# One semaphore for each buffer of gathered rows in the first layer of a two-layer graph network

## The reference, cut to what matters

```python
src, dst = edge_index
h = relu(edge_attr @ W1 + b1)
w_edge = (h @ W2 + b2).reshape(-1, 16, 16)
msgs = einsum('ei,eio->eo', x[src], w_edge)      # x[src]: gathered rows
aggr = segment_sum(msgs, dst, num_segments=n_nodes)
```

## Time and profile before

| what | us |
|---|---|
| median of three runs | 8242.69 |
| lowest, highest | 8239.94, 8244.3 |
| span of the profiled execution, first to last instruction | 8221.3 |
| median less the span: what lies around it | 21.4 |
| first layer, gathers and all, from 60 to 4985 | 4925 |
| second layer's edge loop, about 5080 to 8130 | 3050 |

### The profile page before, as it was taken

One profiled execution on the slowest core, in us unless ns is written; L12 is line 12 of the kernel. 1 busy time (PEld: TensorE's weight loads), 2 busy tenths in 40 slices (PEclk: granted clock), 3 DMA queues, 4 the chain that ended last, 5 costly groups with the idle time before them and its releaser, 6 DMA issues. The chain is left out here.

```text
span 8221.3 us, 191064 instructions
## 1 busy us (share of the span) xinstructions
PE 7349.2 (89%) x52997; PEld 6446.6 (78%) x52997; DVE 6691.0 (81%) x17449; ACT 4457.4 (54%) x8279; POOL 5696.0 (69%) x4866
## 2 busy tenths in 40 slices
PE   7888888888888888888888886999999999999998
PEld 5667676666676666666676765999999999999996
DVE  6777777777777777777777777999999999999997
ACT  3333333333333333333333335888888878778884
POOL 6666666666666666666666664888888888888886
PEclk8999999999999999999999998999999999999999
DMA  2000000000000000000000014444444455554443
GB/s 60 18 17 17 17 17 17 17 17 17 17 17 17 17 18 17 17 17 18 17 17 17 17 23 101 73 75 74 74 75 74 74 73 74 72 74 75 73 75 64
DMA packets 713464, 341.73 MB, mean 42 GB/s; under 512 B 422115, under 2 KB 656599, under 8 KB 713427
## 3 DMA queue, kind: packets, MB, share of 16 engines
q1 hardware_dynamic: 379313, 272.94, 13.1%
q0 software_dynamic: 332928, 64.86, 12.9%
q10 hardware_dynamic: 1186, 3.51, 0.1%
HBM read 307.85 MB, written 32.96 MB: 41 GB/s over the span
## 5 line engine op out<-in xcount | busy, mean ns | idle before, releaser
L802 POOL DMA_INDIRECT xg<-gather_rows,idx x3132 | 3041.9, 971 | 1882.4 <-issue 1848.5
L919 PE MATMUL ps_w<-W2s,hT 128*128 128x256 f32 x12928 | 3240.2, 408 | 37.1 <-issue 36.6
L919 PEld LDWEIGHTS ps_w<-W2s,hT 128*128 128x128 f32 x12928 | 2678.5, 207 | 581.6 <-issue 97.0
L1745 POOL DMA_INDIRECT sums<-total,row x1616 | 2551.0, 1579 | 529.1 <-issue 474.4
L1708 PE MATMUL ps_wide<-hot_col,placed 128*128 128x392 f32 x12928 | 2434.7, 345 | 4.8 <-DVE placed L1544 2.1
L1708 PEld LDWEIGHTS ps_wide<-hot_col,placed 128*128 128x128 f32 x12928 | 2313.6, 196 | 12.2 <-issue 6.9
L841 ACT ACTIVATE hT<-ps_h,b1c 128x512 f32<-128x512 f32 x1616 | 1022.8, 680 | 2302.1 <-PE ps_h L905 2090.8
L1002 DVE TENSOR_TENSOR prod<-ps_w,xg 128x512 f32<-128x512 f32 x1616 | 1098.1, 690 | 969.7 <-remote 599.7
L1544 DVE SCALAR_TENSOR_TENSOR placed<-ps_r,src_r,halves 128x512 fp32r<-128x512 f32 x1616 | 1097.5, 741 | 0.1
L1643 ACT ACTIVATE square<-iota_col,minus_col 128x784 bf16<-128x784 int16 x1212 | 1061.3, 938 | 66.6 <-issue 58.0
L1009 DVE TENSOR_REDUCE msg<-prod 128x32 f32<-128x512 f32 x1616 | 1058.9, 676 | 0.0
(11 more groups left out here) (229 smaller groups left out, 5425.0 us busy)
## 6 DMA issues: line engine op xcount, KB each, us to landing
dst_row<-dst_rows SPq DMA_DIRECT2D x404, 256.0 KB
src_row<-src_rows SPq DMA_DIRECT2D x404, 128.0 KB
xg<-gather_rows,idx POOLq DMA_INDIRECT x3132
q_win<-q_rows SPq DMA_DIRECT2D x404, 96.0 KB
ea<-in_edge_attr SPq DMA_DIRECT2D x404, 64.0 KB
sums<-total,row POOLq DMA_INDIRECT x1616
e<-in_edge_attr SPq DMA_DIRECT2D x404, 32.0 KB
q_rows<-Q SPq DMA_DIRECT2D x12, 768.0 KB, 5.4
```

Source lines behind the costliest of these rows:

```text
L802: pool.indirect_dma_start(xg[r][:, t, :], None, k.rows, bass.IndirectOffsetOnAxis(ap=idx[r][:, t:t + 1], axis=0)).then_inc(xg_in[r][t], 16)
L919: last = pe.matmul(to, hT[half][:, j, col:col + P], k.W2[:, j, :], start=(j == 0), stop=(j == 1 and not with_b2))
L1745: pool.indirect_dma_start(k.sums[t], bass.IndirectOffsetOnAxis(ap=row[r][:, t:t + 1], axis=0), total[r][:, t, :], None, compute_op=ALU.add ...
```

## The change

The 32 gather semaphores become four, one for each buffer. All gathers of a group raise the one of their buffer, by 16 each. VectorE waits for it in unit 0 alone, and for the count of the whole group: `16 * 8 * (lap + 1)`, and for r = 3, which has eight gathers in lap 0 and seven later, `112 * lap + 128`. The wait for `dense_x` stays in unit 3.

```diff
-    xg_in = [[sem(f"xg_in{r}{t}") for t in range(T)] for r in range(RING)]
+    xg_in = [sem(f"xg_in{r}") for r in range(RING)]
...
+    def rows_landed(r, lap):
+
+        return 16 * (T - 1) * lap + 16 * T if r in DENSE else 16 * T * (lap + 1)
...
-                        ).then_inc(xg_in[r][t], 16)
+                        ).then_inc(xg_in[r], 16)
...
                     v.wait_ge(q["wmm"], n + 1)
-                    for t in (2 * u, 2 * u + 1):
-                        if t == T - 1 and dense(r, lap):
-                            v.wait_ge(q["dense_x"], lap)
-                        else:
-                            v.wait_ge(xg_in[r][t], 16 * (lap + 1))
+                    if u == 0:
+                        v.wait_ge(xg_in[r], rows_landed(r, lap))
+                    if u == T // 2 - 1 and dense(r, lap):
+                        v.wait_ge(q["dense_x"], lap)
                     need(v, q["reduced0"], n - 1)
...
-        clear_all(nc, [*q.values(), *ea_in, *(x for r in xg_in for x in r)])
+        clear_all(nc, [*q.values(), *ea_in, *xg_in])
```

## The result

The kernel after takes 8255.97 us (8251.66 to 8262.0, 20 runs), the kernel before 8243.11 us (8239.38 to 8247.07, 20 runs): ratio 1.0017, 95% interval 1.0011 to 1.0023. That is slower, by less than the 0.2% that I had called no change, but twenty runs of each tell it from none: 12.9 us. One of the later executions of the kernel after, among the ten of e14, took 31293 us and stands in no ratio. The profiled execution of the kernel after took 8257.68 us, with a span of 8255.9.

What follows compares the result with a forecast made beforehand. POOL's sequence of gathers with its gaps was taken to bound the first layer; all terms were 0 except up to 3 us off, so span 8221.3 plus 21.4 around it, against the median 8242.69, gave 8240 us, range 8155 to 8275.

Steps and rivals of the forecast that it cites:

- The rest: Outside gathers and row waits: one register instruction 0, fewer semaphores cleared at the layer's end below 3 us, second layer 0.
- Waits that go: VectorE's product waits in the first layer: 2728 of 3232 go, taken as 0 us on the path.
- The two ends that I gave for the waits: Bounds for removing 2728 VectorE waits: nothing to win, or 818 us from sharing out all idle before products.
- the row without a stall: VectorE's stretch from a sum's end at 4952.08 to the next product at 4952.20: 0.12 us at most for all waits.
- POOL: First-layer gathers, order and waits unchanged: 0 us, with bounds of -97 and +101 us from boundary gaps.
- rival 1: Fewer waits shorten the first layer's common stall: 97 us off gives 8146, half of that 8194; chance 0.31.
- rival 4: Time before first-layer products stays under another name, since waits were met long before: 8243 us; chance 0.52 together with the forecast.
- Rival 2: POOL's boundary gap grows towards 2.8 us: up to +101 us, 8344, or 8276 at a third; chance 0.14.
- The 4903 us by groups: First layer as POOL's gathers and gaps: 304 groups of 12.45 us plus 100 of 11.18, against 4925 us.
- rival 3: Unit 0's wait for all eight gathers binds: 404 us and up, 8640 us; chance 0.03.
- the boundary gap between 2.4 and 2.7 us: Sign that the forecast is right: POOL's idle time between groups of gathers stays at 2.4 to 2.7 us.
- the sign of 8 us behind the landing: Sign that the forecast is right: a group's first product starts 8 us or more after the eighth gather's landing.

Runs made afterwards that it cites:

- e14: The changed kernel, unchanged, run again on an occasion with the common stall: 8184.2 us, ratio 1.0011 to the kernel before.
- e13: The kernel before, unchanged, run again on an occasion with the common stall: 8175.4 us, ratio 1.0002.
- e16: The changed kernel plus 41 already-met waits on VectorE between the layers, its second loop back at instruction 857; with the stall: 8160.3 us, ratio 0.9987.
- e11: The kernel before with two more gathers a group into a spare tile nothing reads, without the stall: 8259.3 us, ratio 1.1315.
- e12: The changed kernel with two more gathers a group into a spare tile nothing reads, without the stall: 8265.2 us, ratio 1.1323.
- e5: The changed kernel's one semaphore per buffer, but all 3232 waits of the kernel before kept, without the stall: 7304.1 us, ratio 1.0007.
- e3: The changed kernel plus 41 already-met waits on VectorE between the two layers, without the stall: 7275.8 us, ratio 0.9970.
- e1: The kernel before, unchanged, run again on an occasion without the common stall: 7298.7 us, ratio 1.0000.
- e6: The kernel before, eight semaphores per buffer kept, with all eight waits of a group in front of unit 0, without the stall: 7400.1 us, ratio 1.0138.
- e10: The kernel before with the next group's eight waits moved ahead of the bias of the current group, without the stall: 7289.2 us, ratio 0.9989.

## Why the prediction was wrong

The step that failed is in "The rest": "The second layer: 0". It measured +26.8 us (e13, e14): the loop behind the edits came to lie where its jump back takes 0.12 us longer, and e16, with the loop put back, has 3042.4 us there, 5.3 under e13. I had asked what the edits execute there, which is nothing, and not where they leave the code that follows. No rival had it either.

"Waits that go": 0 for the path, taken because "DVE does not set the pace". As a size it was off by half as much, the other way: the first layer shortened by 13.4 us with the stall (e13, e14). POOL's boundary went from 2.42 to 2.39 us on the mean (-12 us), its short gaps from 0.3074 to 0.3048 (-7 us), its gathers lengthened by 5.9 us. The two ends that I gave for the waits, 0 and 818 us, hold the 30 us measured where DVE does set the pace; nearest to the row without a stall was right, but that row's 0.12 us was not "nothing hidden to win": 0.02 to 0.03 of it went.

"POOL", which I took at 0 between bounds of -97 and +101, stands at -13.8 (idle 1838.1 to 1818.4 us). So rival 1 has the sign of the first layer, at a seventh of its price, and rival 4 (nothing happens) is false: two things happen, and they cancel to +0.1%. Rival 2 has the sign of the whole and not its way: in the first pair the mean boundary went from 2.53 to 2.52 us, not above 2.6. Whether the waits shorten the stall itself or only what stands around it, no run tells apart.

Not shown is that POOL paces the layer. The 4903 us by groups against 4925 seen prove nothing, since the groups' 2.55 us come out of the same idle total; e11 and e12 show only that where POOL does pace, the gain goes. Right were: unit 0's wait for eight costs nothing (e5, without the stall), so rival 3 is out; the boundary gap between 2.4 and 2.7 us. The first product starts 8.2 us after the last gather's end at the least in the first profile of the kernel after and 5.6 in e14, so the sign of 8 us behind the landing was too strict, but the rows are there in both. The range held the time by luck, since the two effects that I had at 0 run against each other. The 8240 rested on 21.4 us around a span which are about 1.75.

The better version is e16: the change, and VectorE's second loop put back in its place, 0.9987 with the stall and 0.9970 (e3) without. It beats both kernels on the first and lies with the kernel after (0.9966) on the second.

## What to carry to other kernels

Price a wait by what its engine has queued when the sequencer meets it: an instruction of one or two waits costs 0.07 to 0.10 us where nothing is queued, a wait about 0.01 us behind an operation of 0.7 us (30 us for the 2728 of this change). Keep them away from the first instruction of a group. When a change adds or removes instructions of an engine, look for the loops that follow in its stream: their jump back may cost 0.1 us more each time round, and a few fillers tell in one run whether that is it. Compare a profiled execution's own time with the kernel's runs before taking a difference of two spans apart.

## What the hardware showed that I had not expected

- The common stall belongs to the occasion, not to the kernel: the same kernel takes 7298.7 us (e1) and 8175.4 us (e13). With it the mean granted clock in the first layer is 0.92 to 0.93, without it 1.00.
- In the stall the sequencers' own instructions stretch to about 0.7 us: before's VectorE has a register instruction of 0.71 us at 2013.08 (elsewhere 0.04) and a wait instruction of 0.69 at 2014.48 (elsewhere 0.02 to 0.05). SyncE's jump back in the first layer takes 0.71 to 0.74 us with the stall and 0.16 without.
- The clock also falls without the stall: e11, where PE waits 624 us for products, shows 0.92 in the first layer and 0.946 over the whole run (e1 0.99), much as e13 (0.93 and 0.948).
- Eight waits in front of one instruction cost 102 us (e6); the same eight, some 4 us earlier in the group's order, leave the kernel 10 us faster than before (e10).
- The jump back of VectorE's second loop takes 0.19, 0.27 or 0.31 us by the loop's place in the instruction stream; the step behind it costs the engine 0.08 to 0.10 us more at the bad places.
